# Batch 1's queries in tiles of their own, the third key buffer zeroed early, results and values ordered earlier

## The chip, the cores and the metric

One core of a Trainium2 chip runs the kernel. The metric is the device time of one execution in microseconds; lower is better. The kernel before took 564.4 us (median of three runs, 562.72 to 565.0).

## What is computed

Two batches of 1024 tokens of 128 numbers go through a "macaron" layer: half a mixture-of-experts feed-forward stage, an attention stage, and again half the same feed-forward stage. Cut to what matters here:

```python
x = x + 0.5 * ffn(layernorm(x))
x = x + attn(layernorm(x))
x = x + 0.5 * ffn(layernorm(x))

def ffn(x):      # 7 routed experts, the 2 likeliest of each token, and a shared one; hidden size 352
    w = top-2 of softmax(x @ wr.T + rb), scaled to sum 1
    return expert(x, shared) + sum over e of w[e] * expert(x, e)

def attn(x):     # 16 heads of 8 columns; the keys are x itself
    v = x @ w_v + v_b
    q = (x @ w_q + q_b) @ w_k.T + k_b
    scores = where(causal, q_h @ x_h.T / sqrt(8), lowest)
    return softmax(scores) @ v_h @ c_proj_w + c_proj_b
```

All arithmetic is in float32; products go through TensorE as a high and a low part.

## The kernel before

The tokens are cut into four chunks of 512; chunks 0 and 1 are batch 0, chunks 2 and 3 are batch 1. Each engine has its own hand-written program, and semaphores order them. The work between the first feed-forward stage and the loop over heads is interleaved by tables that name steps at which an engine does a small job on the side.

**First feed-forward stage.** It has 54 steps (`NQ`), one tile of 128 tokens each: 16 for the shared expert and 38 for the routed ones. GpSimd scatters each routed result to DRAM (L1198). When all scatters of a batch have landed, `results_load` (L1264) brings them back in token order: for batch 0 from SyncE's queue, for batch 1 from ScalarE's, after its last step. For batch 0 ScalarE and VectorE add them up inside the stage; for batch 1 ScalarE weighs them (`weigh_both_act`) and GpSimd adds them (`add_both_pool`, L1139). `FRONT_PE`, `BETWEEN_ACT`, `BEHIND_ACT` and `BEHIND_DVE` (L2080 to L2090) say at which step chunk 0's and chunk 1's normalization for attention (`n_stats`, `n_z`, `n_tr`, `n_hi`, `n_lo`) and their queries (`q`, `q_lo`) are made.

**Queries and keys.** `q_pe` (L1529) multiplies a chunk into a PSUM bank; `q_act` (L1556) adds the bias (tile `q_f`) and rounds to the high part (`q_h`), and `q_dve` for batch 0 or `q_rest_pool` for batch 1 forms the low part (`q_l`). These three tiles have room for two chunks, so chunk 2 reuses the place of chunk 0 and chunk 3 that of chunk 1, behind waits in `q_act`. `queries_sp` (L1590) stores high, high and low part to a DRAM stack (`q_stack`); `keys_store` (L1582) does the same for the keys (`k_stack`), on SyncE's queue for batch 0 and ScalarE's for batch 1. From the stacks a group of four heads is loaded: `queries_load` (L1932) takes 512 KB, `keys_load` (L1938) four blocks of 128 KB that go on the diagonal of a buffer which is zero elsewhere.

**Buffers.** Groups of heads rotate through three key buffers and three query buffers. GpSimd zeroes key buffers 0 and 1 during the feed-forward stage (`wipe_pool`). The third, `keys2`, shares its space with `q_f`, `q_h` and `q_l`; `keys_clear` (L1419) zeroes it by four transfers of 512 KB from rows of the query stack that hold zeros (`keys<-q_stack`), after all queries have been stored.

**Attention.** A softmax row needs its maximum first. `RING_PROLOGUE` is a list of 54 jobs: 38 products of queries and keys of group 0 whose row maxima VectorE takes (L1607 on TensorE, L1760 on VectorE, four PSUM banks in rotation), then two transposes that turn the maxima into rows (`mrow`), and the first 14 maxima of group 1. `rows_load` (L1946) copies the rows into the query tile (`queries<-m_rows`), which releases the score matmuls (`unit_pe`, L1650) and the exponentials (`unit_act`, L1819). `SECOND_PE` (L1719) and `SECOND_DVE` say ahead of which prologue job batch 0's values (`v`, 12 matmuls a chunk, L1509 to L1511) and batch 1's normalization, queries and values are made. `v_act` evicts values, `v_bias_pool` adds the bias on GpSimd.

Then come eight loop bodies, one for each group (six equal ones and two with special ends). `ORDERS` spells the order on TensorE: R a ring job, U a score unit, a the product of one block of probabilities and values (L1679). A body takes the last 24 maxima of the next group and the first 14 of the one after. The first of these 14 waits until that group's keys and queries are loaded; `sp_body` (L1958) issues them as its first act.

**What orders SyncE's queue** is `attn_sp` (L1967): a transfer is issued in program order, behind every wait above it. The lines that matter:

```python
    queries_sp(K, 1, (4, HEADS))
    e.wait_ge(K.FF[0]["mix"], 4)
    keys_load(K, 0, 0, 1)
    e.wait_ge(K.q_st[1], 16 * 3)
    queries_load(K, 0, 0, 1)
    rows_load(K, 0, 0, 0, RING_PROLOGUE.index(("mrow", 0, 0)))
    for c in range(NCH // 2, NCH):
        queries_sp(K, c)
    for c in range(NCH // 2, NCH):
        e.wait_ge(K.k_st[c], 16 * 3)
        e.wait_ge(K.q_st[c], 16 * 3)
    keys_clear(K, 2)
    e.wait_ge(K.cleared, keys_cleared(1))
```

## Time and profile before

| what | value |
|---|---|
| median of three runs | 564.4 us |
| the profiled execution | 568.2 us |
| its span, first to last instruction | 565.9 us |
| mean granted TensorE clock | 0.976 of 2.4 GHz |
| TensorE busy | 520.9 us (92%) |
| VectorE busy | 387.3 us (68%) |
| ScalarE busy | 319.7 us (56%) |
| GpSimd busy | 272.2 us (48%) |
| DMA | 54.64 MB, mean 97 GB/s |

The profiled execution is a run of its own, with 2.3 us around its span, and lies 3.8 us above the median of the others; times within it are compared with each other. TensorE's busy share counts overlapping matmuls, so 92% doesn't mean that it ran at its peak. A wait is shown in brackets behind an instruction: how long the engine stood idle before it, and what released it. "SPq" and "ACTq" are the sequencers of SyncE and ScalarE issuing transfers; the time shown there is that of issuing, and the transfer lands later.

### The profile page before, as it was taken

The numbers are of one execution on the slowest core, as the hardware profiler recorded it, in microseconds if no ns is written. First come the engines' busy times: TensorE is split into PE (matmuls) and PEld (weight loads), VectorE is DVE, ScalarE is ACT, GpSimd is POOL, SyncE is SP. The second block draws the span as 40 slices with busy tenths as digits, with TensorE's granted clock in tenths as the row PEclk, the third lists the DMA queues.
The fourth block names the chain that finished last, engine by engine and source line by source line (L and its number), as shares of the span: only waits on it lengthen the run. The fifth ranks groups of instructions, "written<-read, shape, count | busy, mean of one in ns | idle before, by whom it ended". The sixth has DMA issues, their size and how long they took to land.

```text
span 565.9 us, 11380 instructions
## 1 busy us (share of the span) xinstructions
PE 520.9 (92%) x3574; PEld 405.6 (72%) x3574; DVE 387.3 (68%) x1013; ACT 319.7 (56%) x678; POOL 272.2 (48%) x417
## 2 busy tenths in 40 slices
PE   5998889999887897999999999999999889899995
PEld 2887879988744654656566666665746889899994
DVE  4686635557379884978879798888554776545744
ACT  4563434457344664767767676777776444444643
POOL 8299888766565502122121203030318888854440
PEclk9799989999987998999999999999999999999998
DMA  8921425133760773305050505020001041441414
GB/s 279 295 75 48 115 72 126 50 104 91 220 197 16 221 157 105 128 4 174 2 175 1 178 1 177 0 102 2 3 1 34 30 91 44 105 110 45 128 39 116
DMA packets 41384, 54.64 MB, mean 97 GB/s; under 512 B 6064, under 2 KB 32176, under 8 KB 40560
## 3 DMA queue, kind: packets, MB, share of 16 engines
q1 hardware_dynamic: 31664, 41.13, 25.7%
q0 software_dynamic: 4480, 9.25, 5.0%
q10 hardware_dynamic: 5184, 3.55, 2.2%
q8 instruction: 31, 0.51, 0.4%
q14 instruction: 25, 0.20, 0.1%
HBM read 34.03 MB, written 28.00 MB: 110 GB/s over the span
## 4 chain that ended last, share of the span: by engine, by line
PE 61%; issue 12%; DVE 11%; DMA 9%; SPq 4%; ACT 1%; ACTq 1%; POOL 0%; DVEq 0%; POOLq 0%
PE psum L1650 11%; PE psum L1607 10%; PE psum L1679 10%; PE psum L934 7%; PE psum L920 4%; PE psum L900 3%; PE psum L901 3%; PE psum L902 3%; DVE mxp L1760 2%; PE psum L1610 2%; DMA b_p<-in_attn_c_proj_b 2%; DMA keys<-q_stack 2%; DMA k_stack<-zt_h 1%; PE psum L1635 1%; PE psum L954 1%
## 5 line engine op out<-in xcount | busy, mean ns | idle before, releaser
L1760 DVE TENSOR_REDUCE mxp<-psum 128x1 f32<-128x512 f32 (+3 forms) x304 | 179.2, 655 | 41.0 <-PE psum L1607 32.5
L1819 ACT ACTIVATE probs<-psum 128x512 f32<-128x512 f32 (+1 forms) x304 | 155.2, 579 | 37.4 <-PE psum L1650 34.9
L1650 PE MATMUL psum<-queries,keys 128*128 128x512 f32 (+3 forms) x384 | 123.6, 384 | 1.9 <-DMA queries<-m_rows 1.6
L1866 POOL TENSOR_SCALAR_AFFINE_SELECT probs<-probs 128x512 f32<-128x512 f32 x64 | 40.0, 634 | 177.1 <-ACT probs L1819 177.1
L1607 PE MATMUL psum<-keys,queries 128*128 128x512 f32 (+1 forms) x304 | 115.5, 413 | 8.6 <-DMA keys<-k_stack 3.6
L1001 ACT ACTIVATE silu<-psum 128x352 f32<-128x352 f32 x107 | 49.5, 463 | 94.8 <-PE psum L902 68.0
L1198 POOL DMA_INDIRECT y_rows<-ys,to_row x76 | 74.3, 977 | 52.7 <-DVE ys L1080 28.6
L1044 DVE TENSOR_TENSOR act<-silu,psum 128x352 f32<-128x352 f32 x107 | 55.5, 519 | 64.4 <-ACT silu L1001 35.3
L934 PE MATMUL psum<-wall_f,at 128*128 (+1 forms) x648 | 91.2, 277 | 2.4 <-DVE x L1082 1.2
L1650 PEld LDWEIGHTS psum<-queries,keys 128*128 128x128 f32 x384 | 67.7, 193 | 27.7 <-ACT probs L1819 12.6
L934 PEld LDWEIGHTS psum<-wall_f,at 128*128 128x128 f32 x648 | 81.0, 192 | 4.0 <-issue 2.1
L1607 PEld LDWEIGHTS psum<-keys,queries 128*128 128x128 f32 x304 | 57.8, 193 | 25.1 <-DVE mxp L1760 8.5
L1679 PE MATMUL psum<-probs,vg 128*32 128x512 f32 (+3 forms) x768 | 69.8, 491 | 0.4 <-POOL probs L1866 0.4
L920 PE MATMUL psum<-ident,act 128*128 128x128 f32 x324 | 54.2, 276 | 6.1 <-DVE act L1044 5.1
L1009 ACT COPY at<-psum 128x384 f32<-128x384 f32 x108 | 51.3, 475 | 12.1 <-PE psum L920 8.6
L900 PE MATMUL psum<-wall,zs_h 128*128 x152 | 56.0, 368 | 1.7 <-DVE zs_l L1068 1.7
L901 PE MATMUL psum<-wall,zs_h 128*128 x152 | 49.7, 327 | 0.0
L902 PE MATMUL psum<-wall,zs_l 128*128 x152 | 49.5, 326 | 0.0
L920 PEld LDWEIGHTS psum<-ident,act 128*128 128x128 f32 x324 | 40.8, 141 | 11.8 <-DVE act L1044 8.0
L1679 PEld LDWEIGHTS psum<-probs,vg 128*32 128x32 f32 x768 | 21.0, 109 | 35.5 <-issue 22.0
L1175 POOL DMA_INDIRECT z_rows<-zrow,slots x32 | 34.3, 1072 | 15.7 <-DVE slots L751 10.3
L1175 POOL DMA_INDIRECT z_rows<-zrow_late,slots x32 | 31.2, 975 | 5.8 <-issue 5.8
(240 smaller groups left out, 734.2 us busy)
## 6 DMA issues: line engine op xcount, KB each, us to landing
z_rows<-q_stack SPq DMA_DIRECT2D x12, 682.5 KB, 6.1
keys<-k_stack SPq DMA_DIRECT2D x32, 128.0 KB, 6.4
queries<-q_stack SPq DMA_DIRECT2D x8, 512.0 KB, 6.1
zg_early<-z_rows SPq DMA_DIRECT2D x44, 65.0 KB
yc<-y_rows SPq DMA_DIRECT2D x10, 256.0 KB, 3.4
zg_late<-z_rows SPq DMA_DIRECT2D x32, 65.0 KB
keys<-q_stack SPq DMA_DIRECT2D x4, 512.0 KB, 7.9
q_stack<-q_h SPq DMA_DIRECT2D x6, 256.0 KB, 3.3
```

The source lines that it names most:

```text
L900: e.matmul(dst, zh, weight(K.wall, base, hi, HID), start=True, stop=False)
L901: e.matmul(dst, zh, weight(K.wall, base, lo, HID), start=False, stop=False)
L902: ins = e.matmul(dst, zl, weight(K.wall, base, hi, HID), start=False, stop=True)
L920: ins = e.transpose(bank(K, at_bank(f, q))[:, k * P:(k + 1) * P], K.act[:, q % 2, k * P:(k + 1) * P], K.ident[:, :])
L934: ins = e.matmul(bank(K, Y_BANK)[:, 0:EMB], K.at[:, q % 2, k * P:(k + 1) * P], weight(K.wall_f, base, DN + k * EMB, EMB), start=(k == 0), ...
L1175: e.indirect_dma_start(K.z_dram[f], bass.IndirectOffsetOnAxis(ap=K.slots[:, g:g + 1], axis=0), K.zrow[f][:, t, :], None).then_inc(K.z_sc[t ...
L1198: e.indirect_dma_start(K.y_dram[f], bass.IndirectOffsetOnAxis(ap=K.to_row[:, j:j + 1], axis=0), K.ys[:, j % RING_Y, :], None).then_inc(K.y ...
L1607: ins = e.matmul(dst, K.queries[u][:, i * P:(i + 1) * P], K.keys[u][:, heads[0]:heads[-1] + 1, k0 * P:(k0 + nb) * P], start=True, stop=Tru ...
L1650: ins = e.matmul(slot(K, u, d, n)[:, m * (q1 - q0):(m + 1) * (q1 - q0)], K.keys[v][:, j, kt * P:(kt + 1) * P], K.queries[v][:, q0:q1], sta ...
L1679: ins = e.matmul(bank(K, O_BANK)[32 * j:32 * j + 32, q0 - half * CHUNK:q1 - half * CHUNK], K.vg[:, kt, j, :], probs_of(K, n)[:, j, :], sta ...
L1760: e.tensor_reduce(K.mxp[:, heads[0]:heads[-1] + 1, i, which], scores, AX.X, ALU.max).then_inc(K.A["taken"], 1)
L1819: e.activation(probs_of(K, product)[:, heads[0]:heads[-1] + 1, :], src, ACT.Exp, scale=SCALE).then_inc(K.A["ex"], 1)
```

## The change

It does five things. (1) Chunks 2 and 3 get query tiles of their own (`q_f_late`, `q_h_late`, `q_l_late`), in space that belongs later to probabilities and to the third query buffer; the waits in `q_act` go, and ScalarE waits once, after its first ten exponentials, until batch 1's queries are stored. (2) `keys_clear(K, 2)` moves ahead of the first `rows_load` on SyncE. (3) SyncE waits for batch 1's results to be loaded before it stores heads 4 to 15 of chunk 1's queries and loads group 1. (4) The values of chunk 1 are multiplied ahead of the first maximum, not ahead of the third. (5) The transposes and the query of chunk 1 are made one feed-forward step earlier.

```diff
@@ -384,10 +384,10 @@
                     with ExitStack() as s5:
                         K.keys[2] = sb("keys2", [P, 4, SEQ], F32R, scope=s5)
                     with ExitStack() as s5:
-                        K.q_f = sb("q_f", [P, 2, CHUNK], scope=s5)
+                        q_f0 = sb("q_f", [P, 2, CHUNK], scope=s5)
                         sb("gap2", [P, 2 * CHUNK], scope=s5)
-                        K.q_h = sb("q_h", [P, 2, CHUNK], F32R, scope=s5)
-                        K.q_l = sb("q_l", [P, 2, CHUNK], F32R, scope=s5)
+                        q_h0 = sb("q_h", [P, 2, CHUNK], F32R, scope=s5)
+                        q_l0 = sb("q_l", [P, 2, CHUNK], F32R, scope=s5)
                 with ExitStack() as s4:
                     zt_late = [sb(f"zt_late_{part}", [P, TOKENS], F32R, scope=s4) for part in ("h", "l")]
                     K.zt_h, K.zt_l = ([zt[part], zt[part], zt_late[part]] for part in range(2))
@@ -417,6 +417,15 @@
         sb("below_yc0", [P, 15616], scope=s)
         yc0 = sb("yc0", [P, 2, 2, TPC, EMB], scope=s)
     K.yc = [(yc0, yc1)[c // 2][:, c % 2] for c in range(NCH)]
+    with ExitStack() as s:
+        early = 4 * PROBS_AT[TPC]
+        sb("below_q", [P, (GROUPS + 1) * KT * 32 + early], scope=s)
+        q_h1 = sb("q_h_late", [P, 2, CHUNK], F32R, scope=s)
+        q_l1 = sb("q_l_late", [P, 2, CHUNK], F32R, scope=s)
+        sb("below_qf", [P, 4 * PROBS - early - 4 * CHUNK + KT * 4 * 32], scope=s)
+        q_f1 = sb("q_f_late", [P, 2, CHUNK], scope=s)
+    K.q_f, K.q_h, K.q_l = ([early_q[:, c % 2, :] if c < 2 else late_q[:, c % 2, :] for c in range(NCH)]
+                           for early_q, late_q in ((q_f0, q_f1), (q_h0, q_h1), (q_l0, q_l1)))
     with ExitStack() as s:
         K.o_all = sb("o_all", [P, GROUPS + 1, KT, 32], scope=s)
         K.probs = sb("probs", [P, 4 * PROBS], scope=s)
@@ -1141,9 +1150,9 @@
 
 def q_rest_pool(K, c):
 
-    e, u = K.nc.gpsimd, c % 2
+    e = K.nc.gpsimd
     e.wait_ge(K.A["qh"], c + 1)
-    e.tensor_tensor(K.q_l[:, u, :], K.q_f[:, u, :], K.q_h[:, u, :].bitcast(F32), ALU.subtract)\
+    e.tensor_tensor(K.q_l[c], K.q_f[c], K.q_h[c].bitcast(F32), ALU.subtract)\
      .then_inc(K.A["ql"], 1)
 
 
@@ -1554,22 +1563,17 @@
 
 
 def q_act(K, c):
-    e, u = K.nc.scalar, c % 2
+    e = K.nc.scalar
     e.wait_ge(K.A["q"], c + 1)
-    if c >= 2:
-        e.wait_ge(K.A["ql"], c - 1)
-        e.wait_ge(K.q_st[c - 2], 16 * 3)
-    if c == 3:
-        e.wait_ge(K.q_first, 16 * 3)
-    e.activation(K.q_f[:, u, :], bank(K, Q_BANK[c]), ACT.Identity, bias=K.b_qk[:, 0:1]).then_inc(K.A["qf"], 1)
+    e.activation(K.q_f[c], bank(K, Q_BANK[c]), ACT.Identity, bias=K.b_qk[:, 0:1]).then_inc(K.A["qf"], 1)
     e.wait_ge(K.A["qf"], c + 1)
-    e.copy(K.q_h[:, u, :], K.q_f[:, u, :]).then_inc(K.A["qh"], 1)
+    e.copy(K.q_h[c], K.q_f[c]).then_inc(K.A["qh"], 1)
 
 
 def q_dve(K, c):
-    e, u = K.nc.vector, c % 2
+    e = K.nc.vector
     e.wait_ge(K.A["qh"], c + 1)
-    e.tensor_tensor(K.q_l[:, u, :], K.q_f[:, u, :], K.q_h[:, u, :].bitcast(F32), ALU.subtract)\
+    e.tensor_tensor(K.q_l[c], K.q_f[c], K.q_h[c].bitcast(F32), ALU.subtract)\
      .then_inc(K.A["ql"], 1)
 
 
@@ -1588,12 +1592,12 @@
 
 
 def queries_sp(K, c, heads=(0, HEADS)):
-    e, u = K.nc.sync, c % 2
+    e = K.nc.sync
     done = K.q_first if heads == (0, 4) else K.q_st[c]
     e.wait_ge(K.A["ql"], c + 1)
-    stack_store(e, K.q_dram, 0, c, K.q_h[:, u, :], done, heads)
-    stack_store(e, K.q_dram, 1, c, K.q_h[:, u, :], done, heads)
-    stack_store(e, K.q_dram, 2, c, K.q_l[:, u, :], done, heads)
+    stack_store(e, K.q_dram, 0, c, K.q_h[c], done, heads)
+    stack_store(e, K.q_dram, 1, c, K.q_h[c], done, heads)
+    stack_store(e, K.q_dram, 2, c, K.q_l[c], done, heads)
 
 
 
@@ -1716,7 +1720,7 @@
                            stop=True, skip_group_check=True)
 
 
-SECOND_PE = {0: (("v", 0),), 2: (("v", 1),), 25: (("n_tr", 2),), 30: (("n_tr", 3), ("q", 2)), 35: (("q", 3),), 36: (("v", 2),),
+SECOND_PE = {0: (("v", 0), ("v", 1)), 25: (("n_tr", 2),), 30: (("n_tr", 3), ("q", 2)), 35: (("q", 3),), 36: (("v", 2),),
              38: (("v", 3),)}
 SECOND_DVE = {18: (("n_stats", 2),), 21: (("n_stats", 3),), 26: (("n_lo", 2),), 32: (("n_lo", 3),)}
 UNITS_FROM = max(RING_PROLOGUE.index(("mrow", 0, 1)) + 5, len(RING_PROLOGUE) - AHEAD)
@@ -1849,6 +1853,8 @@
     e.sem_inc(K.A["oev"], 1)
     for n in range(AHEAD):
         unit_act(K, 0, 0, 0, n)
+    for c in range(2, NCH):
+        e.wait_ge(K.q_st[c], 16 * 3)
     for p in range(LOOP3):
         for u in range(3):
             act_body(K, p, u, LOOP)
@@ -1978,18 +1984,20 @@
     e.wait_ge(K.q_st[0], 16 * 3)
     e.wait_ge(K.q_first, 16 * 3)
     queries_load(K, 0, 0, 0)
+    for c in range(NCH // 2, NCH):
+        e.wait_ge(K.y_ld[c], 32)
     queries_sp(K, 1, (4, HEADS))
     e.wait_ge(K.FF[0]["mix"], 4)
     keys_load(K, 0, 0, 1)
     e.wait_ge(K.q_st[1], 16 * 3)
     queries_load(K, 0, 0, 1)
+    keys_clear(K, 2)
     rows_load(K, 0, 0, 0, RING_PROLOGUE.index(("mrow", 0, 0)))
     for c in range(NCH // 2, NCH):
         queries_sp(K, c)
     for c in range(NCH // 2, NCH):
         e.wait_ge(K.k_st[c], 16 * 3)
         e.wait_ge(K.q_st[c], 16 * 3)
-    keys_clear(K, 2)
     e.wait_ge(K.cleared, keys_cleared(1))
     for p in range(LOOP3):
         for u in range(3):
@@ -2077,18 +2085,18 @@
              (LAST, 0): (("x", 0), ("stats", 0), ("x", 1), ("stats", 1), ("z", 0), ("z", 1)),
              (LAST, 1): (("norm_lo", 0), ("norm_lo", 1), ("router", (0, 0)), ("router", (0, 1)), ("places", 0),
                          ("segments", 0), ("lists", (0, 0)), ("lists", (0, 1)), ("lists", (0, 2)), ("lists", (0, 3)))}
-FRONT_PE = {10: (("places", 1),), 47: (("n_tr", 0),), 48: (("q", 0),), 50: (("n_tr", 1),), 51: (("q", 1),)}
-BETWEEN_ACT = [{0: (("query", 0), ("hi0", 2)), 1: (("hi0", 3),), 48: (("q", 0),), 51: (("q", 1),)}, {}]
+FRONT_PE = {10: (("places", 1),), 47: (("n_tr", 0),), 48: (("q", 0),), 49: (("n_tr", 1),), 50: (("q", 1),)}
+BETWEEN_ACT = [{0: (("query", 0), ("hi0", 2)), 1: (("hi0", 3),), 48: (("q", 0),), 50: (("q", 1),)}, {}]
 BEHIND_ACT = [{**{2 * k + 2: (("weights", m),) for k, m in enumerate(ROUTED_WEIGHTS)},
                20: (("tanh", 0),), 42: (("weigh", 0),), 44: (("weigh", 1),), 45: (("n_z", 0),), 46: (("n_hi", 0),),
-               47: (("n_z", 1),), 49: (("n_hi", 1),)},
+               47: (("n_z", 1),), 48: (("n_hi", 1),)},
               {2: (("z", 2),), 3: (("norm_hi", 2), ("norm_hi", 3)), 20: (("tanh", 0),), 39: (("weigh", 0),), 41: (("weigh", 1),), 52: (("results", 1),)}]
 FRONT_DVE = {0: (("router", (0, 0)), ("router", (0, 1))), 1: (("places", 0),), 4: (("segments", 0),),
              5: (("lists", (0, 0)), ("lists", (0, 1))), 6: (("lists", (0, 2)), ("lists", (0, 3))),
              7: (("router", (1, 0)),), 8: (("router", (1, 1)),), 10: (("places", 1),), 14: (("segments", 1),),
              15: (("lists", (1, 0)),), 16: (("lists", (1, 1)),), 17: (("lists", (1, 2)),), 18: (("lists", (1, 3)),)}
 BEHIND_DVE = [{0: (("query", 0),), **{2 * k + 3: (("weights_lo", m),) for k, m in enumerate(ROUTED_WEIGHTS)}, 19: (("small", 0),), 22: (("weights", 0),), 42: (("mix", 0),), 43: (("n_stats", 0),), 44: (("mix", 1),), 45: (("n_stats", 1),),
-               46: (("n_lo", 0),), 48: (("q_lo", 0),), 49: (("n_lo", 1),), 51: (("q_lo", 1),)},
+               46: (("n_lo", 0),), 48: (("q_lo", 0), ("n_lo", 1)), 50: (("q_lo", 1),)},
               {0: (("proj_lo", 2), ("proj_lo", 3)), 1: (("x", 2), ("stats", 2), ("x", 3), ("stats", 3)), 2: (("z", 3),),
                3: (("norm_lo", 2), ("norm_lo", 3)), 4: (("router", (1, 1)),), 8: (("segments", 1),), 9: (("lists", (1, 0)),),
                10: (("lists", (1, 1)),), 11: (("lists", (1, 2)),), 12: (("lists", (1, 3)),), 22: (("weights", 0),),
```

## Rows read from the trace of the kernel before

**Rows 1.** Chain that ended last, in order of time: start us, us, what
```profile
143.48 6.44 DMA k_stack<-zt_h
151.84 4.84 DMA queries<-q_stack
...
198.31 11.64 DMA keys<-q_stack
211.76 5.19 DMA keys<-k_stack
...
234.06 2.29 PE psum L1679 x32
...
263.56 2.29 PE psum L1679 x32
```

**Rows 2.** SyncE's queue in order: start us, us, line, operation, out<-in
```profile
152.26 1.61 SPq L1579 DMA_DIRECT2D q_stack<-q_h  x2
...
159.30 0.35 SPq L1934 DMA_DIRECT2D queries<-q_stack  x1
188.77 1.18 SPq L1955 DMA_DIRECT2D queries<-m_rows  x2
...
197.00 1.73 SPq L1422 DMA_DIRECT2D keys<-q_stack  x4
```

**Rows 3.** TensorE in order, same columns, idle before it and its releaser in brackets
```profile
156.73 0.71 PE L1607 MATMUL psum<-keys,queries 128*128 128x512 f32 x1 [2.47 <-DMA queries<-q_stack]
...
158.20 0.67 PE L1509 MATMUL psum<-wv_h,zt_h 128*128 128x128 f32 x1
...
199.31 2.36 PE L1679 MATMUL psum<-probs,vg 128*32 128x512 f32 x32
...
217.08 0.47 PE L1607 MATMUL psum<-keys,queries 128*128 128x512 f32 x1 [3.62 <-DMA keys<-k_stack]
```

**Rows 4.** Stages: busy us (count) of PE, PEld, DVE, ACT, POOL; clock; DMA share; GB/s
```profile
142.00:146.00 4.00, 4.00 (x30) 3.86 (x29) 1.83 (x5) 2.14 (x5) 0.97 (x2) 1.00 0.93 278
...
157.00:160.00 3.00, 3.00 (x12) 2.16 (x11) 1.39 (x2) 0.00 (x0) 0.03 (x1) 0.50 0.85 263
217.00:222.20 5.20, 5.12 (x21) 3.96 (x21) 2.94 (x5) 2.87 (x6) 0.63 (x1) 0.67 0.00 0
```

**Rows 5.** VectorE in order, prologue of attention
```profile
158.80 0.69 DVE L1760 TENSOR_REDUCE mxp<-psum 128x4 f32<-128x512 f32 x1 [0.19 <-PE psum L1610]
161.15 9.13 DVE L1760 TENSOR_REDUCE mxp<-psum 128x4 f32<-128x512 f32 x16 [1.65 <-PE psum L1607]
...
171.09 0.38 DVE L508 BATCH_NORM_AGGREGATE mv<-stats 128x2 f32<-128x6 f32 x4
```

**Rows 6.** ScalarE and its queue in order, 158 to 200 us
```profile
158.64 2.15 ACTq L1272 DMA_DIRECT2D yc<-y_rows  x4
...
189.38 1.28 ACT L1819 ACT_TABLE_LOAD   x1 [1.44 <-DMA k_stack<-zt_h]
191.91 7.52 ACT L1819 ACTIVATE probs<-psum 128x512 f32<-128x512 f32 x15 [1.25 <-PE psum L1650]
```

**Rows 7.** GpSimd in order, 153 to 171 us
```profile
153.57 0.96 POOL L1198 DMA_INDIRECT y_rows<-ys,to_row  x1 [0.55 <-issue]
...
161.50 3.35 POOL L1552 TENSOR_TENSOR v_all<-v_all,b_v 128x128 f32<-128x128 f32 x8 [4.47 <-ACT v_all L1542]
165.78 5.34 POOL L1139 TENSOR_TENSOR x<-x,yc 128x512 f32<-128x512 f32 x4 [0.93 <-ACT yc L1127]
```

**Rows 8.** Landing times, 130 to 230 us: tile yc, then tile queries
```profile
DMA to landing us min/median/max: 3.4/5.3/5.6
...
DMA to landing us min/median/max: 4.2/4.4/4.6
```

**Rows 9.** End of second feed-forward stage: GpSimd, then SyncE's queue, in order
```profile
551.61 0.96 POOL L1198 DMA_INDIRECT y_rows<-ys,to_row  x1 [1.01 <-DVE ys L1080]
...
554.04 0.92 SPq L1272 DMA_DIRECT2D yc<-y_rows  x2
```

## The prediction

> **What bounds the kernel now.** I read the chain that ended last in order of time first [rows 1]. Around the attention prologue it is no engine but a string of transfers: queries of heads 0 to 3 landing at 156.68, and, after the prologue, the zeroing of the third key buffer (keys<-q_stack, 198.31 to 209.95) and the keys loaded into it behind that (211.76 to 216.95). From 222 us on the chain is the loop's matmuls and repeats every 29.5 us (234.06, 263.56). So I look at two places only: how early the prologue gets going, and what the first loop body loses.
>
> SyncE's queue in order [rows 2] shows the causes. It issues the stores of batch 1's queries last (their landing lets the clear start at 197.00), because the early query tiles lie in the space of the third key buffer. It also stores heads 4 to 15 of chunk 1 at 152.26 and loads for heads 4 to 7 until 159.30, just ahead of batch 1's results, which ScalarE requests at 158.64 [rows 6]. TensorE [rows 3] waits 2.47 us for the queries (156.73), does two maxima, then 12 value matmuls of chunk 1 from 158.20, and VectorE's third maximum comes only at 161.15 after 1.65 us of nothing [rows 5]. At 217.08 TensorE has waited 3.62 us for the third buffer's keys. The stages' table [rows 4] adds that the granted clock is 0.50 (1.2 GHz) in 157 to 160, behind the wait before it, and 0.67 in 217 to 222.2, behind the stall at 213.
>
> **Part 1, the third key buffer zeroed early.** The clear moves from behind batch 1's query stores to a place ahead of the row-maxima load, and the loads into the buffer can then be issued as soon as batch 1's query stores have landed, at the moment where the clear starts now (197.00), less what the prologue gains. They take what they took: clear done at 209.97 (where the loads began), landed at 216.95, so 7.0 us. They land near 204, less part 2, and are wanted where TensorE stopped, 217.08 - 3.62 = 213.5, less the same. Some 9.5 us of cover: nothing of it is left on the path. What the stall cost is read against the next body, not from the idle time alone: the block of 32 probability matmuls starts at 199.31 [rows 3] and again at 234.06 [rows 1], 34.75 us; the next period is 29.50. Difference 5.25 us; I take **5.2**. Ends: 3.6 (only the wait goes, clock and everything else stays) and 5.4.
>
> The clear itself (four transfers) costs 209.97 - 197.00 = 13.0 us of SyncE's queue when alone. Its new start: SyncE now waits for both result chunks of batch 1. ScalarE's four requests take 2.15 us [rows 6] and land 3.4 to 5.3 us after issue [rows 8]; with the requests at 157.0 (below) SyncE goes on at about 162. From the first store (152.26) to the queries load (159.30) it now takes 7.0 us, so the clear starts at 169.4 and is done by 182.4. The row-maxima load is due at 188.77 [rows 2] less part 2, 186.0. Cover 3.6 us, so I cost the clear at nothing; were the cover gone, each us of lateness would be one of time, as nothing else can fill it (the first score matmuls wait for that load).
>
> Batch 1's key stores go out on ScalarE's queue just before the exponentials, and their landing releases the activation table load at 189.38, 1.28 us long, with the first exponential at 191.91 [rows 6]: 191.91 - 189.38 - 1.28 = 1.25 us of slack. The clear's last 3 us may run beside them. Bounds 0 and 1.5; I take 0, as the two overlap only at one end.
>
> **Part 2, the prologue.** (a) The normalization and query of chunk 1 move up one step of the first feed-forward stage. The key store of chunk 1 (issued 143.48, landed 149.92 [rows 1]) runs while the DMA engines are 0.93 busy in 142 to 146 [rows 4], so asking earlier buys little: 0.2 us, bounds 0 and 1 (chunk 0's query stores stay ahead of it in SyncE's queue, which leaves only part of a step). (b) The queries load (151.84, landed 156.68 [rows 1]) no longer has 576 KB of stores issued behind it; such loads land in 4.2 to 4.6 us [rows 8], and this one, 4.84 from the start of its issue, is the slowest. 0.4 us, bounds 0 and 0.6. (c) Chunk 1's values go ahead of the first maximum. Its condition, the last expert tile evicted, holds by then (that tile's scatter starts at 153.57 [rows 7]). The wait begins at 156.73 - 2.47 = 154.26; the 12 matmuls took about 2.4 us at the low clock, so 1.2 at 2.4 GHz, and run inside it until 155.5. The third maximum then follows the second (158.80 [rows 5]) by one VectorE turn of 0.64: 159.44 instead of 161.15, 1.7 us at the low clock. With TensorE pausing 0.6 us in place of 2.47 I expect 2.4 GHz, where the four matmuls of the first two maxima, 156.73 to about 158.8 at the low clock, take 0.8 us less: 2.5 us. Sum of a to c: VectorE's stream moves up by **3.1 us**, bounds 1.7 and 4.1.
>
> (d) That stream is not all: at 171.09 [rows 5] its statistics of chunk 2 meet GpSimd, which must first have added all four results. Now the last scatter ends its issue at 153.57 + 0.96 = 154.5 [rows 7] and the results are requested at 158.64 [rows 6], 4.1 us later, with SyncE's stores and loads on the same engines. Without other traffic the same step takes 554.04 - (551.61 + 0.96) = 1.47 us [rows 9]. Bounds for the request: 156.0 and 158.6; the queries load still runs to 156.1, so I take 157.0, nearer the quiet row. From there: 2.15 issue, 0.6 value copy, 3.35 bias, 5.34 additions [rows 6, 7] and 0.2 of gaps, GpSimd is free at 168.6, against 171.12 now; the wait of 0.93 before the additions goes with the transfer. VectorE's statistics are ready at 171.47 - 3.1 = 168.4. The chain over norm, transposes, queries and the last maxima starts at 168.65 instead of 171.5: **2.8 us** earlier, bounds 0.9 (request unchanged, 158.64: GpSimd free at 170.2) and 3.5. The later key loads for heads 4 to 7 are late next: done by about 172, wanted when the second group's first maximum comes near 185.
>
> The Trainium skill, DMA: Bandwidth & Descriptors, section "Anatomy of one DMA", gives a GpSimd-path transfer a fixed 2.0 us plus its bytes over 436 GB/s; for a scatter of 64 KB that is an estimate of 2.15 us, the request at 156.7, and part 2 limited by VectorE alone, some 0.2 us more gain than mine. The trace's 1.47 us in the quiet case is shorter than that page's figure, and its 4.1 us under traffic far longer; I stay with the rows.
>
> (e) The removed waits on the query copies hid nothing: ScalarE waited there only for TensorE. (f) ScalarE gains one wait, for batch 1's query stores, after its first ten exponentials. Ten take about 5.0 us (15 in 7.52 [rows 6]), from 191.91 to 196.9; the stores are landed at 197.00 [rows 2]. Both ends move together: cost **0.2 us**, bounds 0 and 1.4. Queued behind it are the exponentials that TensorE's three score slots wait for.
>
> **Sum.** 2.8 + 5.2 - 0.2 = 7.8 us. The profiled execution took 568.2 us (span 565.9 and 2.3 around it), so 560.4; it lies 3.8 above the median of the runs, 564.4, from which the same 7.8 gives 556.6.
>
> **Rivals.** *A, only the first body pays.* The request for results stays near 158.6 because the scatters, not SyncE's traffic, were slow; GpSimd then binds, 0.9 us from the front: 0.9 + 5.2 - 0.2 = 5.9, 558.5 us. For it: the loads for heads 0 to 3, 1 MB, stay in flight until 156.7. Against it: the 1.47 us. Chance 0.22. *B, hidden by the next wait.* The stall at 213 gives way to a late exponential: key stores beside the clear land 3 us late, ScalarE starts 1.7 late and stays behind through body 0, and only the wait's 3.6 comes back; 0.9 + 3.6 - 1.7 = 2.8 saved or less, 561.6 or above. For it: 15 exponentials without a gap from 191.91. Chance 0.08. *C, slower.* The clear is still running when the row-maxima load is due. Both are SyncE's; it decides once the clear ends after 186.0, and it makes the kernel slower than before once it ends more than 7.8 us after that, past 193.8. SyncE resuming at 166 and a clear that takes twice its 13.0 us beside key stores gives 173.4 + 26 = 199.4, 13.4 late, less 7.8: 5.6 slower, 570.0. By the same page's section "Queues, rings and completion order" each DMA engine takes a ring's descriptors in order and alternates between rings, which puts the row-maxima load behind the clear and halves the clear's rate while ScalarE's stores run; it gives C its form. Against it: results landing about 162 leave it 11 us. Chance 0.04. *D, the clear is not the late one:* batch 1's query stores, behind which the new loads wait, could be, but their 9.5 us cover speaks against; chance 0.04, about 3 us saved at most.
>
> **Numbers.** Forecast 0.62. The range runs from 10 us saved (all upper bounds, 3.5 + 5.4, and a us of run spread: 562.72 to 565.0) to 3.9 saved, past A: 554.4 to 560.5; under 2 in 10 is left out. A measurement tells about 0.5% (2.8 us) from no change. Faster 0.89 (forecast, A, part of B), within 0.5% 0.07, slower 0.04.
>
> **What would show it.** Right: no wait of TensorE for keys in the first body and 29.5 us from its block of 32 to the next; keys<-q_stack issued near 169 with SyncE free well before the row-maxima load; that load near 186; all 24 value matmuls of batch 0 before the first maximum, VectorE's third maximum at 158 to 159.5, the results requested near 157. Wrong: a TensorE wait on queries<-m_rows longer than now, a table load later than 187.5, a results request still at 158.6, or a gap of ScalarE after ten exponentials.

## The result and the profile after

| | before | changed kernel |
|---|---|---|
| median of 18 runs each | 566.46 us (562.72 to 572.2) | 560.88 us (556.93 to 564.2) |
| ratio, 95% interval | | 0.9906 (0.9885 to 0.9926) |
| the profiled execution | 568.2 us | 556.93 us |
| its span | 565.9 us | 555.1 us |

The change gains 0.94%, 5.3 us (the interval is 4.2 to 6.5 us). The sign is as predicted; 560.88 lies 0.4 us past the end of the range. The two profiled executions differ by 11.3 us, because that of before is longer than 13 of the 18 runs and that of the changed kernel is its shortest; so the stages are compared below over several profiles of each kernel, and never by the span of one.

The page's first part, of the changed kernel:

```profile
span 555.1 us, 11378 instructions
...
PE 516.0 (93%) x3574; PEld 402.7 (73%) x3574; DVE 386.5 (70%) x1013; ACT 319.7 (58%) x678; POOL 273.0 (49%) x417
```

SyncE's queue in order, changed kernel (answers to [rows 2]; L1583 stores, L1940 and L1948 load, L1431 is the clear, L1961 the row maxima):

```profile
148.39 0.34 SPq L1940 DMA_DIRECT2D queries<-q_stack  x1
160.57 1.62 SPq L1583 DMA_DIRECT2D q_stack<-q_h  x2
...
166.43 1.84 SPq L1431 DMA_DIRECT2D keys<-q_stack  x4
182.77 1.38 SPq L1961 DMA_DIRECT2D queries<-m_rows  x2
...
192.07 1.82 SPq L1948 DMA_DIRECT2D keys<-k_stack  x4
```

SyncE now rests from 148.7 to 160.6, until batch 1's results are in. The clear starts at 166.43 instead of 197.00, and the four loads of keys for the third buffer are issued from 192.07 on. Before, they were issued from 210.35 on, the last of them at 211.76 [rows 1].

TensorE in order, changed kernel (answers to [rows 3]):

```profile
153.97 0.27 PE L1520 MATMUL psum<-wv_h,zt_l 128*128 128x128 f32 x1
154.09 0.44 PE L1611 MATMUL psum<-keys,queries 128*128 128x512 f32 x1
...
186.34 0.47 PE L1654 MATMUL psum<-queries,keys 128*128 128x512 f32 x1 [2.52 <-DMA queries<-m_rows]
...
195.70 2.36 PE L1683 MATMUL psum<-probs,vg 128*32 128x512 f32 x32
```

The 24 value matmuls now run straight into the first maximum: no wait for the queries is left. The stall of 3.62 us for the third buffer's keys is gone too; the next block of 32 starts at 225.29 by the chain, 29.6 us after 195.70, where it was 34.75. But the first score matmul has waited 2.52 us for the row maxima. The same wait was shorter before (the row of before's TensorE, not among those above):

```profile
191.41 0.47 PE L1650 MATMUL psum<-queries,keys 128*128 128x512 f32 x1 [1.58 <-DMA queries<-m_rows]
```

VectorE and GpSimd in order, changed kernel (answer to [rows 5] and [rows 7]):

```profile
154.79 10.32 DVE L1764 TENSOR_REDUCE mxp<-psum 128x4 f32<-128x512 f32 x18 [2.67 <-PE psum L1614]
165.03 0.86 DVE L514 BATCH_NORM_STATS2 stats<-x 128x6 f32<-128x128 f32 x4
```

```profile
152.22 0.96 POOL L1207 DMA_INDIRECT y_rows<-ys,to_row  x1 [0.55 <-DVE ys L1089]
...
160.77 5.34 POOL L1148 TENSOR_TENSOR x<-x,yc 128x512 f32<-128x512 f32 x4
```

Eighteen maxima without a gap, and additions that end at 166.1. The last scatter ends its issue at 153.2, and the results are requested 1.5 us later, in ScalarE's stream (answers to [rows 6]):

```profile
154.70 2.07 ACTq L1281 DMA_DIRECT2D yc<-y_rows  x4
...
176.22 2.92 ACTq L1583 DMA_DIRECT2D k_stack<-zt_l  x1
179.17 1.56 ACTq L1583 DMA_DIRECT2D k_stack<-zt_h  x1
180.78 0.69 ACT L1568 ACTIVATE q_f_late<-psum,b_qk 128x512 f32<-128x512 f32 x1 [4.59 <-issue]
...
185.97 1.28 ACT L1823 ACT_TABLE_LOAD   x1 [1.52 <-DMA k_stack<-zt_h]
187.26 1.08 ACT L1823 ACTIVATE probs<-psum 128x512 f32<-128x512 f32 x2
```

Here is what the prediction priced at nothing: two of batch 1's key stores take 2.92 and 1.56 us to issue, and chunk 3's query stands 4.59 us behind them. Before, all six stores took 0.53 to 0.63. The stages (columns as in [rows 4]) show the clock:

```profile
152.00:157.00 5.00, 4.91 (x31) 3.40 (x29) 2.33 (x6) 0.19 (x1) 3.47 (x3) 1.00 0.31 96
157.00:160.00 3.00, 2.50 (x7) 1.03 (x6) 3.00 (x7) 2.15 (x7) 2.53 (x7) 0.96 0.92 266
186.30:191.00 4.70, 4.66 (x15) 3.65 (x15) 3.09 (x6) 4.03 (x7) 2.12 (x5) 0.64 0.92 293
```

The granted clock is 1.00 in the stretch with the first maxima and 0.96 in 157 to 160, where it was 0.50 before. But it is 0.64 behind the 2.52 us wait, where it was 1.00 before (189 to 197).

The price can be read from rows already shown. From the issue of the first row maxima to the first block of 32, it was 199.31 - 188.77 = 10.5 us before and is 195.70 - 182.77 = 12.9 us now: 2.4 us lost, against some 5.2 us gained in the period behind it.

All profiles of a kernel can be laid over each other from one moment, the issue of chunk 0's first key store on SyncE, which no edit touches (134.31 in the profile of before, 133.28 in that of the changed kernel). Times in us from there, worked out from each trace; "rows" is the first issue of queries<-m_rows, "third rows" the third, after which the loop is the same in all:

```
profile           results   additions  clear    rows    third   between
                  requested end        issued           rows    the two
before            24.3      36.8       62.7     54.5    118.2   63.7
before_again      25.2      37.1       62.6     54.4    117.6   63.2
before_third      25.0      37.4       63.1     54.9    117.9   63.0
before_fourth     25.1      36.8       61.5     53.2    118.3   65.1
changed kernel    21.4      32.8       33.2     49.5    110.5   61.0
same1             21.6      33.0       33.4     49.7    110.3   60.7
same_again        22.2      33.7       34.1     50.4    111.4   61.1
same_fourth       22.1      33.5       33.9     51.7    110.6   58.8
```

Means: first rows 54.3 to 50.3 (4.0 saved; 5.0, 4.0 and 1.5 in the pairs of the two first profiles, of before_again and same_again, and of before_fourth and same_fourth), the rest to the third 63.8 to 60.4 (3.4 saved), together 7.3 us.

The stretch between first and third rows splits at the loop's first two blocks of 32. "Overlap" is the time from the issue of batch 1's first key store on ScalarE's queue to the end of the clear's last packet, by the packet records of the traces; both moments count from chunk 0's first key store:

```
profile           rows to    block to   clear's end   first key   overlap   wait of the first
                  block      block      in the trace  store                 score matmul
before            10.5       34.7       behind them   47.4        none      1.58
before_again      10.6       34.1       behind them   47.4        none      1.60
before_third      10.6       33.9       behind them   47.9        none      1.59
before_fourth     10.6       36.0       behind them   46.0        none      1.61
changed kernel    12.9       29.5       47.6          42.3        5.3       2.52
same1             12.6       29.5       47.1          42.5        4.6       2.23
same_again        13.0       29.6       47.9          43.1        4.8       2.57
same_fourth       10.8       29.5       47.6          44.1        3.6       1.52
```

So the gain of the period is there every time, and the loss ahead of it in three of four.

### The profile page after: what moved, and what is told of

Read it like the earlier page. It is cut to its first block, busy times and chain, and to the rows that moved or that the text cites. A ratio compares the mean times of both kernels' runs of the same rounds, so it can differ in the third digit from the quotient of the medians.

```text
span 555.1 us, 11378 instructions
## 1 busy us (share of the span) xinstructions
PE 516.0 (93%) x3574; PEld 402.7 (73%) x3574; DVE 386.5 (70%) x1013; ACT 319.7 (58%) x678; POOL 273.0 (49%) x417
## 4 chain that ended last, share of the span: by engine, by line
PE 64%; POOL 15%; DVE 8%; DMA 5%; issue 4%; ACT 1%; ACTq 1%; SPq 0%; POOLq 0%; DVEq 0%
PE psum L1654 13%; PE psum L1611 12%; PE psum L1683 11%; POOL z_rows L1184 10%; PE psum L943 7%; PE psum L929 3%; POOL idle L1194 3%; PE psum L909 3%; PE psum L910 3%; PE psum L911 3%; DVE mxp L1764 3%; PE psum L1614 2%; DMA b_p<-in_attn_c_proj_b 2%; PE psum L1639 1%; PE psum L963 1%
## 5 line engine op out<-in xcount | busy, mean ns | idle before, releaser
L1611 PE MATMUL psum<-keys,queries 128*128 128x512 f32 (+1 forms) x304 | 116.7, 421 | 2.3 <-DVE mxp L1764 1.7
L1611 PEld LDWEIGHTS psum<-keys,queries 128*128 128x128 f32 x304 | 59.0, 197 | 17.9 <-DVE mxp L1764 7.6
L1018 ACT COPY at<-psum 128x384 f32<-128x384 f32 x108 | 51.2, 474 | 9.9 <-PE psum L929 9.7
L1683 PEld LDWEIGHTS psum<-probs,vg 128*32 128x32 f32 x768 | 21.0, 109 | 35.5 <-issue 22.7
L1184 POOL DMA_INDIRECT z_rows<-zrow,slots x32 | 34.7, 1086 | 14.1 <-DVE slots L760 8.7
## 6 DMA issues: line engine op xcount, KB each, us to landing
keys<-q_stack SPq DMA_DIRECT2D x4, 512.0 KB, 11.4
```

Source lines behind the costliest of these rows:

```text
L1184: e.indirect_dma_start(K.z_dram[f], bass.IndirectOffsetOnAxis(ap=K.slots[:, g:g + 1], axis=0), K.zrow[f][:, t, :], None).then_inc(K.z_sc[t ...
L1611: ins = e.matmul(dst, K.queries[u][:, i * P:(i + 1) * P], K.keys[u][:, heads[0]:heads[-1] + 1, k0 * P:(k0 + nb) * P], start=True, stop=Tru ...
L1683: ins = e.matmul(bank(K, O_BANK)[32 * j:32 * j + 32, q0 - half * CHUNK:q1 - half * CHUNK], K.vg[:, kt, j, :], probs_of(K, n)[:, j, :], sta ...
```

## The experiments

Kernels of one group were measured together and share their runs of before; the medians of before were 565.04, 566.33, 565.94, 570.63 and 567.45 us in the five groups. Each ratio is against the before of its own group. Times "at" some us in this section count from chunk 0's first key store, as in the tables above, where they stand below 130.

```
run             group median us  ratio (95% interval)
same1           1     561.73     0.994  (0.9912 to 0.9967)
clear_only      1     575.2      1.018  (1.0157 to 1.0204)
no_clear        1     563.01     0.9976 (0.9949 to 1.0004)
no_ywait        1     571.66     1.0117 (1.0085 to 1.0149)
no_values       2     560.45     0.9905 (0.9873 to 0.9937)
no_step         2     562.1      0.9926 (0.9896 to 0.9956)
places_only     2     566.57     1.0009 (0.9985 to 1.0034)
pool_clear      2     557.93     0.9872 (0.9825 to 0.9918)
before_again    3     565.83     1.0013 (0.9991 to 1.0036)
same_again      3     560.91     0.9923 (0.9893 to 0.9952)
wait_at_clear   3     559.95     0.9907 (0.9875 to 0.9939)
pool_again      4     562.52     0.9867 (0.9822 to 0.9913)
pool_no_wait    4     565.88     0.9934 (0.9904 to 0.9964)
pool_no_values  5     559.35     0.9863 (0.9833 to 0.9894)
```

**The changed kernel again**, unchanged, as the measure for its parts.

> The changed kernel again, unchanged, for a second profile. Between the two profiles at hand the time from chunk 1's first key store to the first body's block of 32 fell by 2.6 us and the first body by 5.2, 7.8 in all, while the medians of 18 runs differ by 5.6. Theory S (the profiled pair was a slow run of before and a fast one of after, and the rest differs by chance elsewhere): again about 29.5 us between the blocks of 32 and the block 62 to 63 us behind the first key store (133.28 to 195.70 = 62.4), with spans that differ outside of 133 to 226 us. Theory V (the prologue's gain itself varies): the block of 32 comes 64 us or more behind the first key store.

0.994; with 0.9923 later and 0.9906 at first, repeats of one kernel lie 0.34% apart, so smaller differences between edits are not read from the times.

**The clear left where it was.**

```diff
-    keys_clear(K, 2)
     rows_load(K, 0, 0, 0, RING_PROLOGUE.index(("mrow", 0, 0)))
...
         e.wait_ge(K.q_st[c], 16 * 3)
+    keys_clear(K, 2)
     e.wait_ge(K.cleared, keys_cleared(1))
```

> The change with the clear left behind the query stores. Theory T: the front keeps its gain (row-maxima load issued some 5 us earlier against the first key store) and the first body its stall of 3.6 us and period of 34.7. If the clear beside batch 1's key stores is what cost 2.3 us in the changed kernel, here the row-maxima load lands in 2.6 us (not 3.4), the key stores take 0.6 us each to issue, and the saving is about 5 us: ratio 0.991. If the clear costs nothing there: 2.6 us, ratio 0.995.

0.9976, a smaller gain than either expectation. It is 0.36% behind same1 of the same group, hardly more than repeats differ by, so the stages must tell. In its trace the first rows come at 50.8 us, near the changed kernel's, but the third at 114.2: the stretch between them is 63.4, as before, and TensorE waits 2.92 us for keys<-k_stack. So by the stages about half of the 7.3 us hangs on the early clear, and 3.8 us are saved without it. The times show 0.24% (1.4 us) of these 3.8; their interval reaches 2.9 us.

**The early clear by itself**, with the late places, and parts 3, 4 and 5 undone:

```diff
-    for c in range(NCH // 2, NCH):
-        e.wait_ge(K.y_ld[c], 32)
     queries_sp(K, 1, (4, HEADS))
...
-SECOND_PE = {0: (("v", 0), ("v", 1)), 25:
+SECOND_PE = {0: (("v", 0),), 2: (("v", 1),), 25:
...
-FRONT_PE = {10: (("places", 1),), 47: (("n_tr", 0),), 48: (("q", 0),), 49: (("n_tr", 1),), 50: (("q", 1),)}
+FRONT_PE = {10: (("places", 1),), 47: (("n_tr", 0),), 48: (("q", 0),), 50: (("n_tr", 1),), 51: (("q", 1),)}
```

> Own query places and the early clear alone; results, values and chunk 1's step as before. Theory T (each part pays for itself): 5.2 us less than before in the first body, nothing in front of it: ratio 0.991. Theory C (without the wait for results, the clear runs beside them): the clear starts near 160 and the results, requested at 158.6, land some 3 to 6 us later than now; the row-maxima load is then as late or later than before, and the ratio is 0.995 to 1.002.

1.018: slower than before, by 10 us, and past both expectations. **Only the wait taken away** (the first two lines of that diff) tells why.

> The change without SyncE's wait for batch 1's results. Theory T (removing traffic made the results come early): results requested as late as before, 4 us behind the last scatter's issue, and landing beside the clear; the front loses 2 to 5 us, ratio 0.995 to 1.0. Rival (the scatters are slow by themselves, and the gain came from the earlier step): request stays 1.5 us behind the last scatter's issue and ratio stays at 0.990.

1.0117, past both expectations too. ScalarE of this kernel, in order:

```profile
161.68 2.52 ACTq L1281 DMA_DIRECT2D yc<-y_rows  x4
...
178.31 4.78 ACT L1136 ACTIVATE yc<-yc,w 128x128 f32<-128x128 f32 x16 [12.99 <-DMA yc<-y_rows]
```

Its DMA queues in 160 to 180 us (packets, MB, share of the engines; q1 is SyncE's, q10 ScalarE's), and the issues with their landing times:

```profile
q1 hardware_dynamic: 508, 3.06, 63.9%
q10 hardware_dynamic: 2112, 1.05, 26.5%
...
keys<-q_stack SPq DMA_DIRECT2D x4, 512.0 KB, 11.9
yc<-y_rows ACTq DMA_DIRECT2D x4, 256.0 KB, 16.3
```

The changed kernel's results, in 155 to 162 us:

```profile
yc<-y_rows ACTq DMA_DIRECT2D x4, 256.0 KB, 3.8
```

Without the wait the clear is issued 0.65 us behind the results (at 162.33 of the trace), and the same megabyte takes 16.3 us instead of 3.8. The first rows come at 65.1 us instead of 50.3. The results are a megabyte in packets of 0.5 KB; SyncE's 508 packets average 6 KB, but the clear's own, 128 of them, are of 16 KB in the packet records. The queue with small packets gets the small share: in 170 to 173 us the clear's queue moved 0.52 MB and the results' 0.03, and 0.44 MB of the results came only in 176 to 180, as the clear ended (177.7). So the wait is not there only to let the results be requested early; without it the early clear is a loss.

**The late places and ScalarE's new wait by themselves** (the clear late as in no_clear, and parts 3 to 5 undone as in clear_only):

> Own query places and ScalarE's wait behind its first ten exponentials alone, all else as before. Predicted cost 0.2 us, bounds 0 and 1.4: ratio 1.000, at most 1.003. A larger ratio would show that this wait or the new places eat part of the gain.

1.0009, the third rows at 118.4 against a mean of 118.0 before: the places cost nothing that can be measured.

**The values of chunk 1 back ahead of the third maximum** (the SECOND_PE lines of clear_only's diff):

> The change with chunk 1's values back ahead of the third maximum. Theory T: the third maximum comes 1.0 us (2.4 GHz) to 2.4 us (1.2 GHz) later, and all that follows with it, since in the changed kernel VectorE has no idle time between the first maximum and its 18th: ratio 0.992 to 0.994 (0.990 with the values early). Rival (GpSimd's additions bind, so the stream had slack): no change, 0.990.

0.9905, no slower than the changed kernel, though the first rows come later, at 51.2 us. The third come at 110.0 all the same. Its trace shows one way in which that happens: the key stores start later too, at 43.5 us, and only 3.6 us of the clear run beside them. TensorE waits 1.52 us for the row maxima, not 2.52, and the block of 32 comes 10.7 us behind the first rows, not 12.9.

**The step of chunk 1's query undone** (the FRONT_PE lines and their partners in the other tables):

> The change with chunk 1's transposes and query back one step later. I had costed this at 0.2 us. In the profile of the changed kernel the loads of group 0 came 2.8 us earlier against the first key store than before. Theory T2 (the step carries that): here they come back to 16 us behind the first key store (149.99 - 134.31), first maximum 2 to 2.8 us later, ratio 0.994 to 0.995. Theory as predicted (the engines are saturated, the step buys 0.2): ratio 0.990.

0.9926. The key loads for heads 0 to 3 are issued 14.9 us from the key store, 12.9 to 13.8 with the step. But the first maximum starts at 21.1 us, within the changed kernel's 20.8 to 21.6, and the first rows come at 49.9, within its range too: the earlier loads gain nothing that shows.

**The clear by GpSimd instead of DMA.** If the clear's bytes delay the key stores, a clear without bytes must take that away.

```diff
-    keys_clear(K, 2)
     rows_load(K, 0, 0, 0, RING_PROLOGUE.index(("mrow", 0, 0)))
...
-    e.wait_ge(K.cleared, keys_cleared(1))
+    e.wait_ge(K.cleared, WIPES)
...
+def clear_pool(K, parts):
+    e, n = K.nc.gpsimd, SEQ // 2
+    if parts[0] == 0:
+        e.wait_ge(K.q_st[0], 16 * 3)
+        e.wait_ge(K.q_first, 16 * 3)
+        e.wait_ge(K.q_st[1], 16 * 3)
+    for part in parts:
+        j, half = divmod(part, 2)
+        e.memset(K.keys[2][:, j, half * n:(half + 1) * n].bitcast(F32), 0.0).then_inc(K.cleared, 1)
...
             norm_rstd_pool(K, 1, 3)
+            clear_pool(K, range(0, 5))
             outputs_pool(K)
             q_rest_pool(K, 2)
+            clear_pool(K, range(5, WIPES))
```

> The change with the third key buffer zeroed by eight GpSimd fills (five behind chunk 3's norm, three behind chunk 2's low part) in place of 2 MB of transfers. Theory T (the clear beside batch 1's key stores costs 2.3 us between the row maxima and the first body): key stores issue at 0.6 us each, the row-maxima load lands in 2.6 us, 1 to 2.3 us less than the changed kernel: ratio 0.986 to 0.989. Rival (GpSimd's fills of 0.54 us each delay its additions of batch 1's bias or low part, which the query stores need): ratio 0.990 or above.

0.9872, the fastest kernel so far, as the expectation that blamed the clear's transfers had it. ScalarE, TensorE and GpSimd of it, in order:

```profile
179.81 0.60 ACTq L1595 DMA_DIRECT2D k_stack<-zt_l  x1
...
189.50 1.09 ACT L1835 ACTIVATE probs<-psum 128x512 f32<-128x512 f32 x2 [1.27 <-PE psum L1666]
```

```profile
188.99 0.47 PE L1666 MATMUL psum<-queries,keys 128*128 128x512 f32 x1 [1.60 <-DMA queries<-m_rows]
```

```profile
174.80 2.39 POOL L1443 MEMSET keys<- 128x512 f32 x5
...
181.13 1.46 POOL L1443 MEMSET keys<- 128x512 f32 x3
```

and the stage behind the first score matmul, as in [rows 4]:

```profile
189.00:193.00 4.00, 4.00 (x19) 2.97 (x20) 3.41 (x8) 3.42 (x8) 0.65 (x1) 1.00 0.86 248
```

The stores issue in 0.60, the wait is 1.60 as before, the clock 1.00, and ScalarE has its 1.27 us of slack back. The third rows come 59.4 us behind the first. The block of 32 comes 11.4 us behind the first rows, 1.6 us sooner than in the changed kernel's profile, but still 0.8 later than before; that rest has no run of its own.

**Repeats against the spread**: before twice more, the changed kernel once more.

> The kernel before, unchanged, to see its own spread and what stands outside the prologue. Theory S (chance): ratio 1.000 within its interval, first key store anywhere between 133 and 137.5 us, as in the nine variants, 99.7 us from there to the second body's block of 32. Theory F (the change also delays the first stage): first key store at 134 to 135 us again, as in the first profile (134.3) and in the variant with the places alone (134.8), against a mean of 136.4 in the variants that move steps.

> As before_again: theory S a first key store anywhere from 133 to 137.5 us, theory F 134 to 135; 99.7 us from there to the second body's block of 32.

> The changed kernel, a third profile. Theory S: 91.9 us from the first key store to the second body's block of 32, first key store anywhere from 133 to 137.5, ratio near 0.990 (0.9906 and 0.994 so far). Theory F: first key store 136 to 137.

Before against itself 1.0013; the changed kernel 0.9923. Their stages stand in the tables above; before_third is a single run, 567.26 us. The first key store of before comes at 136.20 and 135.91 of the trace here, so its 134.31 at first was chance, and the change does not delay the first stage.

**The results wait moved down to the clear**: SyncE's stores and loads go ahead of the results as before, but the clear doesn't.

```diff
-    for c in range(NCH // 2, NCH):
-        e.wait_ge(K.y_ld[c], 32)
     queries_sp(K, 1, (4, HEADS))
...
+    for c in range(NCH // 2, NCH):
+        e.wait_ge(K.y_ld[c], 32)
     keys_clear(K, 2)
```

> The change with SyncE's wait for batch 1's results moved down, to stand only ahead of the clear: chunk 1's later query rows and group 1's loads go out as before. Without any wait the results took 16.3 us to land beside the clear. Theory T (two separate gains: the clear kept off the results, 10 us and more; and the request 2.7 us earlier): results requested 24.2 us behind the first key store as before, landed 5.7 us later, the clear starting near 30, some 2 us worse than the changed kernel: ratio 0.993 to 0.995, not 1.01. Rival (only the clear matters): 0.990.

0.9907, as the rival of this expectation had it. The results are requested at 24.8 us, as late as before, and VectorE stands behind GpSimd's additions:

```profile
170.79 0.87 DVE L514 BATCH_NORM_STATS2 stats<-x 128x6 f32<-128x128 f32 x4 [2.25 <-POOL x L1148]
```

The first rows come at 54.5, where they were before. Yet the third come at 113.2, 58.7 behind them: here the clear, issued at 31.7 us, ends at 43.1, before the key stores, which wait for the later front and start at 47.3. The stage says 2.5 us worse than the changed kernel, the times say no worse. Part of that is the choice of execution: the profiled one, 564.46 us, is the longest of its six, the others taking 558.88 to 561.51. The next runs put the question again, without the clear's transfers in them.

**Four kernels on the question of the wait and the values**: before and the changed kernel once more (a single run each, 570.51 and 565.59 us), and the GpSimd clear, as it is, without the results wait, and without the early values.

> The kernel before, fourth profile. From the first key store to the third row-maxima load before took 118.2, 117.6, 117.9 us and the changed kernel 110.5, 110.3, 111.4; the rest of the span differs the other way by 1 to 2 us. In six of ten profiles of the changed kernel and its variants, TensorE's clock falls to 1.2 GHz behind its wait for rows at 480 us in the second feed-forward stage (1.6 to 2 us lost), in none of four of before. Theory S (chance): sooner or later before shows it too. Theory F: never; 312 us from the third load to the end.

> The changed kernel, fourth profile: 110.3 to 111.4 us from the first key store to the third row-maxima load; theory F: the clock falls behind the wait for rows near 480 us, 313 to 314 us to the end; theory S: either way.

> The changed kernel with GpSimd's fills in place of the transfers, again, against 0.9872 [0.9825, 0.9918]: from the first key store to the third row-maxima load 109.2 us as before (changed kernel 110.7), ratio 0.986 to 0.990.

> GpSimd's fills, without SyncE's wait for batch 1's results. With the transfers this wait was worth 13 us, as the results landed 16.3 us after their request beside the clear. Theory T: with no clear on the DMA engines, what is left is the earlier request: results requested 24 to 25 us behind the first key store (21.7 with the wait), landed 5.5 us later, first row-maxima load at 54.5 (49.8), and 58.7 us from there to the third: 113.2 us, ratio 0.991 to 0.993. Rival: the later query rows and group 1's loads hold nothing up; 109.2, ratio 0.987.

> GpSimd's fills, and chunk 1's values back ahead of the third maximum. Theory T (the values' gain of 1.6 us at the first row-maxima load was eaten by the clear beside the key stores): with no clear it passes through; first key store to third row-maxima load 110.8 us or more against 109.2 and 110.2 with the values early, ratio 0.989 to 0.990. Rival (the gain is lost in the first body whatever clears the buffer, as ScalarE or VectorE binds there): 109.2 to 110.2, ratio 0.987.

The GpSimd clear repeats: 0.9867. Without the wait it is 0.9934, slower by 0.7% in the ratio and 3.4 us in the medians, and in the stage the third rows come at 112.0 instead of 109.2 and 110.2, 2.3 us later. Without the early values it is 0.9863, and the third rows come at 110.1. So the wait pays by the earlier request too, and the early values show no gain.

The pair of the fourth group shows the collision from the other side. In same_fourth the key stores and the first rows came late by chance (44.1 and 51.7 us), only 3.6 us of the clear ran beside the stores, the wait for the rows was short, and the stretch behind it is the shortest of the changed kernel, 58.8:

```profile
191.55 0.47 PE L1654 MATMUL psum<-queries,keys 128*128 128x512 f32 x1 [1.52 <-DMA queries<-m_rows]
```

## Why the prediction was right in its two gains and too high in its sum

The step that failed is "I cost the clear at nothing", with its term for batch 1's key stores, "Bounds 0 and 1.5; I take 0, as the two overlap only at one end". It measured 2.1 to 2.4 us in three profiles of four. The prologue's gain was set too low by 1.2 us and hides much of that. The rest of the miss is a base of three runs, and 1.7 us that no stage shows.

**The third buffer (5.2 us).** The gain is as predicted: clear early, keys early, no stall, and from block to block 29.5 us instead of 34.7 on average, 5.1 saved. no_clear shows it from the other side. The cost beside it is the failed step. The clear was issued at 33.2 us from the key store (my 169.4 was 35.1). Its four transfers landed 8.2 to 13.6 us after their issue, and its last packet ended at 47.6, near my 182.4 (48.1). But the key stores had moved up more than forecast: 47.4 less 2.8 would have been 44.6, and they began at 42.3. So the clear ran beside them for 5.3 us, where I had written "last 3 us". Two of the stores took 4.5 us to issue in place of 1.2, and their last bytes moved 2.7 us behind the issue of the row-maxima load (0.1 before). The wait for the row maxima was 2.52 in place of 1.58, and the clock behind it fell to 0.64.

The size can be read by laying profiles together. From the first rows to the block of 32 it is 10.5 to 10.6 us in all four of before and 12.6 to 13.0 in the three of the changed kernel with 4.6 us of overlap or more; no_step, with 4.6, has 12.9. Where the overlap was 3.6 us, about what I had forecast, it is 10.8 (same_fourth) and 10.7 (no_values), and where the clear was over it is 10.6 (wait_at_clear). The term measures **2.1 to 2.4 us** at an overlap of 4.6 us or more, above its upper bound of 1.5, and near nothing at 3.6. Pricing the overlap I had written down at nothing was thus nearly right; taking it for the overlap that would come was not. Of the cost, 0.6 to 1.0 us is the later start of the first score matmul, 3.3 to 3.6 us behind the issue of the rows instead of 2.6. How the remainder divides between the lower clock and ScalarE's lost slack, no run shows. Of 63.8 us before, 60.4 remain on average: 3.4 saved where the sum had 5.2 - 0.2.

**The prologue (2.8 us).** It gave 4.0, over the upper bound of 3.5. The queries' wait vanished, because the value matmuls fill all of it and the first maximum starts 0.1 us behind them; the request came 1.5 us behind the last scatter, as the quiet row had it. The estimate of 157.0 is 22.7 us from the key store; it was 21.4 to 22.2. The prediction calls that quiet row's 1.47 us shorter than its estimate of 2.15 us for a scatter; this is so from the end of the scatter's issue, and from its start it is 554.04 - 551.61 = 2.43 us. Both streams, VectorE's and GpSimd's, moved by nearly 4 us (additions end at 37.0 before, 33.3 after) and still meet: 165.93 and 166.40 in the profile. Term (a), 0.2 for the step, and term (f), 0.2 for ScalarE's wait, hold within the spread (no_step, places_only). Of (b) and (c), the parts cannot be told apart in time: without the early values the first rows come some 0.9 us later, and nothing is left of that at the third rows. With the clear's transfers in the kernel, the smaller overlap takes it back. pool_no_values shows that this isn't the only thing that does; what else does is open.

By the stages the change saves 7.3 us, near the forecast of 7.8, by two errors that offset each other. That the sum came so close is luck.

**The wait for the results.** I priced it only as an earlier request. pool_no_wait puts that at about 2.3 us, but the larger part was its shelter from the clear: no_ywait's 16.3 us landing. This is rival C's mechanism, a clear that collides, at another victim: I set it against the row-maxima load, and it struck the results. In the change as made it did not come to pass.

**From 7.3 to 5.3 us.** The rest is lost where the prediction had no term. In the four profiles of each kernel, the mean time ahead of the first key store goes from 135.5 to 135.7 us and that behind the third rows from 312.9 to 313.6. That leaves 6.4 us by the spans; the other 1.1 lies between four profiles and the medians of 18 runs. Over all profiles the first stretch is 133.3 to 137.5 us long and the second 311.3 to 316.1, so both spread by more than the missing 2 us. Part of this goes by the group: the four profiles of the fourth, before among them, have 314.6 to 316.1 us behind the third rows, the other 15 have 311.3 to 314.0.

One thing was seen only with edits on. In the second feed-forward stage TensorE waits 1.2 to 2.1 us for gathered rows in 13 of the 14 profiles of the changed kernel and its variants, and 1.7 to 1.95 in the five of before and places_only. In 7 of the 14 the clock fell behind that wait, in none of the five. Outside the fourth group, those seven took 313.3 us behind the third rows on average and the four with the clock kept 311.6, so the fall costs about 1.7 us. TensorE of the changed kernel, clock kept, then of same1, clock lost; the second row is the same six matmuls:

```profile
476.24 0.41 PE L963 MATMUL psum<-ident,zg_early 128*128 128x128 f32 x2 [1.69 <-DMA zg_early<-z_rows]
477.85 0.83 PE L943 MATMUL psum<-wall_f,at 128*128 x6
```

```profile
479.21 0.41 PE L963 MATMUL psum<-ident,zg_early 128*128 128x128 f32 x2 [1.83 <-DMA zg_early<-z_rows]
...
481.18 1.49 PE L943 MATMUL psum<-wall_f,at 128*128 x6
```

Half of 1.7 would be some 0.8 of the 2 us. Whether the change makes the fall likelier or it is chance stays open, and so does the remainder.

**The number.** I took the saving from 564.4, the median of the three runs shown; over 18 runs before is 566.46. From there 7.8 gives 558.7 and the measured ratio 561.1. So of the 4.3 us between 556.6 and 560.88 about 2.1 are the base, 0.5 is the stages' sum (7.8 against 7.3), and 1.7 are the loss just named (7.3 against 5.6, the difference of the medians). The upper end of the range had counted none of them.

## What to carry to other kernels

A transfer that is moved off one wait must be checked against every transfer in flight at its new place, on other queues too, and above all small-packet ones: here one wait ahead of a 2 MB fill decided between 0.9% faster and 1.2% slower. Where an idle engine can write zeros, try that before moving zeros by DMA: eight GpSimd fills of 3.85 us in all gave 0.987 twice, where the early transfers gave 0.991 to 0.994; the intervals touch, the stages agree. And when a front moves up, the later work moves into what was clear of it. Here 3.6 us of overlap cost nearly nothing and 4.6 us or more cost 2: recompute all overlaps at the new times, for a gain at its upper bound too.

## What was not expected of the hardware

The results' megabyte, in 0.5 KB packets, took 16.3 us beside the clear's 16 KB packets and 3.8 without them, a slowdown by four. The clear suffered less: the median landing of its four transfers was 7.9 us in the kernel before, where it had the engines nearly to itself, 11.9 beside the results, and 11.4 in the changed kernel, beside group 1's loads and the key stores. The Trainium skill, DMA: Bandwidth & Descriptors, section "Queues, rings and completion order", says that a DMA engine goes round-robin between queues, one packet at a time. With packets of such different size that would give the bytes to the queue with the large ones, and the trace agrees in direction: in 170 to 173 us of no_ywait the two queues moved 48 and 50 packets, but 0.52 and 0.03 MB; in 167 to 170, 42 and 298 packets, 0.43 and 0.15 MB. Whether the profile's packets are those of that page, no run here shows.

The load also shows at the issuing end: a 256 KB store took ScalarE's queue 2.92 us to issue beside the clear, and 0.60 in the kernel without it.

TensorE's clock fell to 1.2 GHz behind the wait for the row maxima in the four profiles where that wait was 2.23 to 2.57 us, and stayed at 2.4 GHz in the other 15, where it was 1.52 to 1.62. The length of a wait alone doesn't tell elsewhere. At the wait for the queries (1.90 to 2.68 us in the four profiles of before, places_only and clear_only) the clock fell every time. It also fell once in the middle of the prologue in every profile, at 166.6 to 175.6 us, where in most of them no single wait was above 1.5 us. Near 480 us it fell behind 1.76, 1.83, 1.88, 2.05, 2.06, 2.09 and 2.13 us and stayed behind 1.76, 1.94, 1.95 and 1.97.
